# Causal attention with 8-wide heads: the next unit's first scores issued ahead of this unit's shift on TensorE

## What is computed

```
q = heads(x @ Wq + bq); k = heads(x @ Wk + bk); v = heads(x @ Wv + bv)    # 16 heads of 8
att = einsum('bhqd,bhkd->bhqk', q, k) * 8 ** -0.5
att = where(tril(ones((256, 256))), att, -inf)
y = einsum('bhqk,bhkd->bhqd', softmax(att), v)
```

## Time and profile before

| | |
|---|---|
| median of three runs | 2622.39 us (2617.27 to 2626.8) |
| the profiled execution, its own time | 2621.8 us |
| its span, first to last instruction | 2619.7 us |
| busy share of the span | TensorE matmul 84%, VectorE 70%, ScalarE 51%, GpSimd 47% |
| TensorE's mean granted clock | 0.918 of full speed |
| stretch of the attention `l1s` | first join of maxima at 415.6 us, last at 738.7 us |

### The profile page before, as it was taken

The page is one execution under the profiler, slowest core; times in us unless marked ns, Lnnn a source line. Parts: engine busy times, 40 slices in busy tenths (PEclk is TensorE's granted clock), DMA queues, the critical chain, the costliest instruction groups (busy, mean ns, idle before and its releaser), DMA issues. The chain is left out here.

```text
span 2619.7 us, 68614 instructions
## 1 busy us (share of the span) xinstructions
PE 2204.5 (84%) x22578; PEld 1684.8 (64%) x22578; DVE 1823.9 (70%) x5026; ACT 1339.4 (51%) x2821; POOL 1244.3 (47%) x1952
## 2 busy tenths in 40 slices
PE   5859987999978678599999977899677999997845
PEld 3648984666656567477777755666554888885623
DVE  6975545666669745488888857677684666666977
ACT  3435552333334446355555545444544888883456
POOL 4446526555434465477777644333351434333333
PEclk9969998999989779799999989899876999998978
DMA  8022210000000223100000000000000121110000
GB/s 309 2 112 79 72 46 26 14 13 12 8 2 0 89 79 88 54 13 11 10 9 10 5 20 9 2 0 1 1 17 23 57 65 57 65 49 14 1 9 25
DMA packets 81633, 96.69 MB, mean 37 GB/s; under 512 B 16560, under 2 KB 60729, under 8 KB 79353
## 3 DMA queue, kind: packets, MB, share of 16 engines
q1 hardware_dynamic: 73216, 77.12, 9.1%
q0 software_dynamic: 8192, 16.79, 2.2%
HBM read 56.51 MB, written 37.36 MB: 36 GB/s over the span
## 5 line engine op out<-in xcount | busy, mean ns | idle before, releaser
L1931 DVE TENSOR_TENSOR l2f_experts_h_lo<-l2f_experts_h,l2f_experts_h_hi 128x512 fp32r<-128x512 f32 x256 | 186.7, 751 | 130.3 <-ACT l2f_experts_h_hi L1857 126.4
L991 POOL TENSOR_TENSOR a_pm<-a_pt,tri_post 128x256 f32<-128x256 f32 x256 | 179.1, 727 | 94.4 <-ACT a_pt L647 94.3
L785 DVE TENSOR_REDUCE l1s_negm<-l1s_s 128x3 bf16<-128x384 f32 x256 | 131.3, 557 | 108.2 <-PE l1s_s L476 108.1
L1872 ACT ACTIVATE l2f_experts_h<-l2f_experts_f,ahead 128x512 f32<-128x512 f32 x256 | 174.7, 687 | 51.3 <-DVE l2f_experts_h_lo L1931 45.9
L1969 POOL TENSOR_TENSOR l2f_acc<-l2f_experts_tmp,l2f_acc 128x512 f32<-128x512 f32 x64 | 82.8, 1294 | 228.3 <-DVE l2f_experts_tmp L1901 228.3
L785 DVE TENSOR_REDUCE a_negm<-a_s 128x2 bf16<-128x512 f32 x256 | 164.6, 685 | 32.7 <-PE a_s L476 32.1
L647 ACT ACTIVATE l1s_pt<-l1s_st 128x768 f32<-128x768 f32 x128 | 96.9, 811 | 158.5 <-PE l1s_st L511 158.5
L1857 ACT ACTIVATE l2f_experts_h_hi<-l2f_experts_h 128x512 fp32r<-128x512 f32 x256 | 154.2, 631 | 0.0
L647 ACT ACTIVATE a_pt<-a_st 128x1024 f32<-128x1024 f32 x128 | 126.5, 1066 | 2.8 <-PE a_st L511 2.8
L663 ACT ACTIVATE a_q_hi<-a_pa 128x256 fp32r<-128x256 f32 x64 | 24.6, 384 | 189.8 <-PE a_pa L442 189.8
L1792 PE MATMUL l2f_experts_f<-l2f_x_hi,l2f_experts_w_hi 128*128 128x512 f32 x256 | 100.7, 393 | 6.4 <-POOL l2f_experts_w_lo L1959 6.4
(11 more groups left out here) (549 smaller groups left out, 7056.7 us busy)
## 6 DMA issues: line engine op xcount, KB each, us to landing
expert_rows<-zeros SPq DMA_DIRECT2D x16, 1056.0 KB, 16.9
l2f_experts_wrow<-weights_by_expert SPq DMA_DIRECT2D x64, 256.0 KB, 3.1
l0f_w<-in_l0f_w SPq DMA_DIRECT2D x8, 640.0 KB
l0f_x_in_sb<-expert_rows SPq DMA_DIRECT2D x72, 64.0 KB
expert_rows<-l0f_y SPq DMA_DIRECT2D x72, 64.0 KB, 1.6
l1f_x_in_sb<-expert_rows SPq DMA_DIRECT2D x72, 64.0 KB
expert_rows<-l1f_y SPq DMA_DIRECT2D x72, 64.0 KB
ahead<-in_l2f_w SPq DMA_DIRECT2D x6, 512.0 KB, 4.7
```

The source lines that it names most:

```text
L785: dve.tensor_reduce(dst, src, AX.X, ALU.max, negate=True).then_inc(max_done, 1)
L991: last = pool.tensor_tensor(pm[:, par, heads_, kt, :], pt[:, par, heads_, kt * (T + P):kt * (T + P) + P], K["tri_post"][:].unsqueeze(1).br ...
L1872: act.activation(h[:, j], psum_f[j][:], ACT.Gelu, bias=col(e, j)).then_inc(h_ready, 1)
L1931: dve.tensor_tensor(h_lo[:, pos % 2, j], h[:, j], h_hi[:, pos % 2, j].bitcast(F32), ALU.subtract)\
```

## The change

In each step, where `before` is true, TensorE now issues `score_mask(nn, 0)` and `scores(nn, 0)` first and `shift(n)` after them. All instructions and all waits stay as they were; only TensorE's order differs. For the other attentions the order stays.

```diff
@@ emit, on TensorE
+                if before and inside(nn):
+                    score_mask(nn, 0)
+                    scores(nn, bn, un, posn, 0)
                 if inside(n):
                     shift(n, pos)
                 if U == 1 and turn_now:
                     turn(b2, b2)
-                if inside(nn):
-                    if before:
-                        score_mask(nn, 0)
+                if inside(nn) and not before:
                     scores(nn, bn, un, posn, 0)
                 if U == 4 and inside(nn) and (per_unit or un == 0):
                     project_v(nn, bn, un)
```

## The result

The changed kernel takes 2663.85 us (median of four runs, 2654.8 to 2668.38), against 2621.69 us before; the ratio is 1.0161, 95% interval 1.0135 to 1.0187. It is slower by 1.6%, some 42 us, where 36 were forecast. Its profiled execution took 2663.2 us with a span of 2661.2 us.

What follows compares the result with a forecast made beforehand. In this stage VectorE waits for TensorE, in a ring where each item waits for the one before. Full batches at +2.55 us give 33.2, with 1.5, 1.0 and 0.2 together +35.9: 2658 us, range 2634 to 2670.

Steps and rivals of the forecast that it cites:

- Ordinary step: Steps away from the turn: 4.69 us between first scores against 4.82, 0.13 less.
- term for tile shape: From shift to `values` in each step: the change of tile shape adds 0.10 us, bounds 0 and 0.21.
- Into the turn: Step u = 2 to a batch's turn: 7.19 us between first scores against 5.97, 1.22 more.
- Behind the turn: From the turn's first scores (u = 3) to the next: 6.75 us against 5.16, 1.59 more, set by GpSimd's line.
- 0.14 us of slack: Kernel before, behind the turn: GpSimd's line to the second unit's keys has 0.14 us to spare.
- a fallen clock: Rival, whole stage: TensorE idles more and its clock drops to 1.2 GHz; +160 us and more, 2820; chance 0.04.
- The sum: All batches of the stage together: +35.9 us, 2.55 us for a full batch, giving 2658 us.
- GpSimd's line off the path: Rival, at the turn: GpSimd's line does not bind, the turn costs 0.08 instead of 1.59; +15 us, 2637; chance 0.12.
- The faster case: Rival, ordinary steps: VectorE's ring closes early, 3.88 us a step in place of 4.82; -45 us, 2577; chance 0.07.

Runs made afterwards that it cites:

- experiment 5: Changed kernel with the query mask laid six times both at the turn and in the step after it; 2650.91 us, ratio 1.0114.
- experiment 3: Changed kernel with GpSimd's keys laid out ahead of values and gather in the turn's step; 2641.28 us, ratio 1.0071.
- experiment 9: Kernel before, TensorE's old order, with GpSimd's keys ahead of values and gather in the turn's step; 2617.41 us, ratio 0.9986.
- experiment 6: Changed kernel with shift's mask issued first in each step, shift first at the turn, GpSimd's keys before values and gather there; 2594.69 us, ratio 0.99.
- experiment 8: Changed kernel with the shift first again at the turn and GpSimd's keys ahead of values and gather there; 2617.66 us, ratio 0.999.
- experiment 1: Changed kernel with the new order in all steps but the turn, where the shift is issued first again; 2631.59 us, ratio 1.0039.

## Why the prediction was right

The direction, the place and nearly the size came out, but the size by two errors that cancel in part.

- **Ordinary step, -0.13 us.** Measured -0.14 (4.82 to 4.68). TensorE's own line takes the place of the join, and the second mask no longer finds TensorE idle. The term for tile shape, taken as 0.10 between 0 and 0.21, measures 0.08: shift to `values` is 613.22 - 612.46 = 0.76 in the changed kernel, less the 0.68 to a mask:

```profile
612.46 0.83 PE L511 MATMUL l1s_st<-ident_bf,l1s_negm 128*128 128x128 bf16 x12
...
613.22 0.86 PE L549 MATMUL l1s_nd<-l1s_pt,l1s_vb 128*32 128x256 f32 x16
...
614.01 0.39 PE L461 MATMUL l1s_s<-mask_q,ident_bf 128*128 128x256 bf16 x2
```

  The rule of the Trainium skill (TensorEngine Tiling (Array Packing), Key Properties) that a change of tiling mode drains TensorE agrees with these 0.08 us; no run here shows that they are a drain.
- **Into the turn, +1.22 us.** Measured +0.98. The mis-sized piece is the 0.49 us from `turn` to the second mask: it held a wait for VectorE that the new order does not have. Before, the second mask starts at 572.77, right behind the end of VectorE's maxima at 572.71; in the changed kernel the maxima are over ahead of `turn`, and the piece is 0.28 us (623.38 to 623.66):

```profile
571.69 1.02 DVE L785 TENSOR_REDUCE l1s_negm<-l1s_s 128x3 bf16<-128x384 f32 x2 [0.74 <-PE l1s_s L476]
```

```profile
621.60 1.01 DVE L786 TENSOR_REDUCE l1s_negm<-l1s_s 128x3 bf16<-128x384 f32 x2
...
623.38 0.44 PE L430 MATMUL l1s_pa<-ident,l1s_xn 128*128 128x128 f32 x2
...
623.66 0.38 PE L461 MATMUL l1s_s<-mask_q,ident_bf 128*128 128x256 bf16 x2
```

- **Behind the turn, +1.59 us.** Measured +1.27 at full clock in the changed kernel's looped batches (6.43), +1.27 or +1.47 in experiment 5 (6.43 and 6.63). The chain was right link by link, and experiment 3 shows it to be the binding one; three of its links are 0.05 to 0.16 us shorter than the rows they were taken from, the copy of the values among them, which starts 1.40 us after the exponentials' start and not 1.51. In the two turns without a gather the forecast left +0.54 of this term, and nothing came: 5.18 and 5.19, TensorE's own line, against 5.21 and 5.09 before. The 0.14 us of slack that the working gave GpSimd's line before the change stands: the 0.19 us that experiment 9 took off that interval are VectorE's join.
- **The clock.** The forecast summed at 1.00 and gave a fallen clock 0.04, reasoning from a mean: at 14.04 us busy of 20 it had held. That was the step that failed. The changed kernel is busier than that in each 20 us from 420 to 780 (16.18 us or more), and the clock still fell in seven turns and four of the steps behind them. With the later rise in the first batch it costs 13.4 us here (experiment 5).
- **The sum.** +35.9 us forecast; at full clock the stage loses 28.2, and the clock adds 13.4, 41.6 in all. That the time came within 6 us of the forecast is luck: the order was taken 8 us too dear and the clock at nothing. The range held the time, with 6 us to its upper end, because its upper end stood for other unknowns.
- **The rivals.** GpSimd's line off the path (2637) is what experiment 3 made of the kernel: 2641, with three fallen clocks in it. The faster case asked for TensorE to be ready when the first maxima end; taking 0.44 us of mask off its line, as experiment 6 does, gave 0.44 us a step, once the turn as a whole lost nothing (6.53 and 4.11 against 5.98 and 5.16). At that rival's price of 6 us per 0.1 us of a step this is 26 us; from experiment 8 to experiment 6 it was 23.0.

## What to carry to other kernels

An instruction moved ahead of another on the same engine takes its waits with it: list what the mover waits for in the rarest step, not only in the ordinary one, since what it now holds back may be the head of a chain through three other engines. Before moving a piece look for parts of what it passes that need nothing late; here the shift's mask, kept in the wait in which it stood before the change, made the same idea pay. And when an engine's order opens a wait, look at what stands in order on the engines behind it: one line of GpSimd's order was worth 22 us in one kernel and nothing in the other.

## What the hardware showed that was not expected

The clock of TensorE fell in a stretch with a high mean share of busy time. In the changed kernel it fell after waits of 1.52 us, in the midst of matmuls, and not in every batch: the scores at 485.70 had the same wait of 1.52 us ahead of them and the interval behind them is 6.43, those at 604.04 have 7.54. It also fell after waits of 1.12 to 1.32 us, and in experiment 1 after 0.84 and 0.85 us, while a wait of 1.17 us (scores at 492.13 of the changed kernel) was followed by no fall: the length of the wait alone does not decide. Ten more matmuls in one wait moved the fall to the next one, of 1.18 us; ten in each of the two held the clock at 1.00 and made the kernel 13 us faster. Which turns lose the clock is not explained by these runs.

An instruction of VectorE's that does the same work took twice as long beside one order of GpSimd's pieces as beside the other: the join of the maxima at the turn, 0.34 us and 0.16 us (experiment 9). In the kernel before, this was worth 0.19 us of a looped batch's interval.
